# GpSimd waits for the landing of seven gathered blocks one gather later in a graph layer

## Chip, cores and metric

One core of one Trainium2 chip. The metric is the time of one execution on the device, in microseconds (us); less is better. The kernel before took 3305.88 us, the median of 3 runs (3302.12 to 3306.97).

## What is computed

Two layers over 6250 nodes of 256 features (x), in f32. The first, which matters here, is a relational graph layer over 200000 edges, sorted by their end node (dst); each edge has a source node, one of 16 types and a weight:

```python
def _L0_gnn_ref(feat, norm, weight, w_comp, h_bias, loop_weight, src, dst, etypes):
    w_full = jnp.einsum('rb,bdo->rdo', w_comp, weight)
    x_rel = jnp.einsum('nd,rdo->rno', feat, w_full)
    msg = x_rel[etypes, src] * norm
    agg = jax.ops.segment_sum(msg, dst, num_segments=N)
    out = agg + h_bias + feat @ loop_weight
    return jax.nn.relu(out)

    x = x + _L0_gnn_ref(_layernorm(x, axis=-1), edge_weight1, ...)
    x = x + _L0_ffn_ref(_layernorm(x, axis=-1)[None], ...)[0]
```

The second is a mixture of 16 experts of which each node uses 2. The change doesn't touch it.

The end nodes are drawn as 6250 times the square of a uniform number, so low nodes have many more edges than high ones. The host hands the nodes over in reverse order: the kernel meets the sparse end first, and a tile of 256 nodes has few edges at the start of the graph layer and very many at its end.

## The kernel before

The kernel has stages in order: loading and normalising the rows, tables and coefficients of the edges (both before 196 us), the graph layer (`graph_layer`, to about 2699 us), routing, experts, and combining. In the graph layer the edges stand in 1568 blocks of 128. For each block the 128 source rows of 256 f32 (128 KB) are gathered from DRAM (`d.feat`) into a slot of a ring in SBUF, `rows`, of RB = 56 slots. The nodes are in windows of WIN = 16; each pair of a block and a window that it touches is a step, 1960 steps in all, and U = 7 steps are a turn, 280 turns. TW = 16 windows are a tile of 256 nodes.

**GpSimd** issues the gathers (line 1060), one indirect DMA for each block, in sections of GB = 14. Ahead of a section (lines 1043 to 1056) it waits until TensorE has done the turn after which the ring has room for the section (`s_P`, `free[q]`): room means that all blocks more than 42 below the first of the section are used. Then it copies the list of source nodes of the next section (`list_in`, line 1035). Every seven gathers (QB = 7) count their landing on one semaphore, `s_row[at // QB]`, so the ring has eight of them, used in turn; a gather adds 16. Ahead of the first gather of each seven stands `landed` (line 1038), which waits until the seven before have landed, all of them, and then increments `s_paced`. The first 28 gathers are issued in the stage before (line 712), with no such wait, and partly in a run with nothing between them.

**SyncE** waits for the same semaphores in their order, seven blocks after seven, and adds 7 to `s_in` each time (`rows_in`, line 1016).

**VectorE** builds for each turn the matrix S of selected coefficients (line 1147), in four buffers; it waits there for the turn of TensorE that used the buffer last. After the turn that ends a tile it also does the work on the nodes of that tile (`nodes`, lines 1093 to 1117).

**TensorE** goes through the turns. In each it waits for S and for the rows of the turn's blocks (`s_in`), and does 7 products of S with a slot of the ring into PSUM (line 1282; 14 matmul records in the profile). Where a turn is the first of a new tile it does the product of the former tile with the basis weights first (`tile_product`: lines 1211, 1224, 1192, 1232, 1237, 1201). **ScalarE** moves the windows out of PSUM (lines 1340, 1342) and serves the tile products with copies (line 1354).

Of the kernel before, what the change touches and what calls it, by code (L numbers as in the profile page):

```python
# [79 lines left out]
GB = 14  # L80
QB = 7
# [89 lines left out]
def later(i):  # L171

    return not isinstance(i, int) or i > 0
# [784 lines left out]
def graph_layer(nc, d, a, ctl, pairs, room, wend, srcT, dstS, wgtS, coefS, ident, wb, lw, hb, gw, s_w, logit, choice, mean, rstd, idx, rows, s_row):  # L958
# [5 lines left out]
    with ctx:  # L964
# [38 lines left out]
        @blk.sync  # L1003
        def _(e):


            for c in range(HC):
                e.dma_start(wb[:, c, :, :], a["L0_gnn_weight"].rearrange("b (c p) o -> c p b o", p=P)[c, :, :, :]).then_inc(s_w, 16)
            e.dma_start(lw[:, :, :], a["L0_gnn_loop_weight"].rearrange("(c p) o -> p c o", p=P)).then_inc(s_w, 16)
            e.dma_start(hb[:, :], a["L0_gnn_h_bias"].partition_broadcast(P)).then_inc(s_w, 16)  # L1010
            e.dma_start(choice[0][:, :], a["L0_ffn_gate_b"].partition_broadcast(P)).then_inc(s_gb, 16)
            e.dma_start(gw[:, :, :], a["L0_ffn_gate_w"].rearrange("(c p) e -> p c e", p=P)).then_inc(s_w, 16)
            def rows_in(i):
                for q in range(RB // QB):
                    e.wait_ge(s_row[q], 16 * QB * (i + 1))
                    e.sem_inc(s_in, QB)  # L1016
            i0 = 0
            for k, (t, n, i1) in enumerate(CHUNK):
                with e.Fori(i0, i1) as i:
                    rows_in(i)  # L1020
                e.wait_ge(s_S, t + n)
                c = slice(t * U * B, (t + n) * U * B)
                e.dma_start(coefS[:, c], d.coef[:, c]).then_inc(s_late[k], 16)
                i0 = i1
            with e.Fori(i0, NBLK // RB) as i:
                rows_in(i)

        @blk.gpsimd
        def _(e):
            ch = Chain(e, s_pool)  # L1030
            regs = [e.alloc_register(f"room{q}") for q in range(IB)]
            last = NBLK // (IB * GB) - 1

            def list_in(group, q):
                ch.add(e.tensor_copy(idx[:, q * GB:(q + 1) * GB], srcT[:, bass.ds(group * GB, GB)]))

            def landed(i, n):

                e.wait_ge(s_row[n % RB // QB], i * (IB * GB // RB * 16 * QB) + (n // RB + 1) * 16 * QB)
                e.sem_inc(s_paced, 1)  # L1040

            def blocks(i):
                e.load(regs, room[0:1, bass.ds(i * IB, IB)])
                free = [e.snap(r, min_val=1, max_val=TURNS) for r in regs]
                for q in range(0 if later(i) else EG, IB):
                    if later(i) or q >= RB // GB:

                        e.wait_ge(s_P, free[q])
                        e.sem_inc(s_turn, 1)
                    if later(i) or q > EG:  # L1050
                        ch.wait()
                    if q < IB - 1 or not isinstance(i, int) or i < last:
                        list_in(i * IB + q + 1, (q + 1) % IB)
                    else:
                        e.sem_inc(s_turn, 1)
                    for u in range(GB):
                        at = (q * GB + u) % RB
                        if u % QB == 0:
                            landed(i, q * GB + u - QB)
                        e.indirect_dma_start(rows[:, at * H:(at + 1) * H], None, d.feat, bass.IndirectOffsetOnAxis(ap=idx[:, q * GB + u:q * GB + u + 1], axis=0)).then_inc(s_row[at // QB], 16)  # L1060
            e.iota(choice[1][:, :], [[1, X]], base=-X, channel_multiplier=0, allow_small_or_imprecise_dtypes=True).then_inc(s_xno, 1)
            e.iota(node.rearrange("p (m n) -> p m n", m=2), [[1, 2], [2, WIN // 2]], base=0, channel_multiplier=0, allow_small_or_imprecise_dtypes=True).then_inc(s_node, 1)
            blocks(0)
            with e.Fori(1, last) as i:
                ch.base, ch.n = IB * i - EG, 0
                blocks(i)
            ch.base, ch.n = IB * last - EG, 0
            blocks(last)

        @blk.vector  # L1070
# [1003 lines left out]
```

## Time and profile before

| | |
|---|---|
| median of 3 runs | 3305.88 us (3302.12 to 3306.97) |
| the profiled execution, its time | 3305.05 us |
| its span | 3303.3 us |
| mean granted TensorE clock | 0.847 of full speed |
| from the first gather of line 1060 to the start of the last | 197.35 to 2653.84 us |

Engines in the profile: PE is TensorE (PEld its weight loads), DVE is VectorE, ACT is ScalarE, POOL is GpSimd, SP is SyncE; a q behind the name is the engine's queue of instructions. Times are us, or ns where said. A wait is put down to what ended it; "issue" is idle time in which the engine waited for nothing that the profile shows. A gather's own duration on POOL is that of its issuing; its bytes move and land later, and appear as DMA traffic.

### The profile page before, as it was taken

Reading aid. Unit: us, or ns where it says so; the run is one execution under the profiler, and the core shown is the slowest. Engines: PE = TensorE matmul, PEld = TensorE weight load, DVE = VectorE, ACT = ScalarE, POOL = GpSimd, SP = SyncE. Lnnn points to the kernel's source line nnn. Section 1 sums busy time; section 2 is a strip of 40 time slices with the busy share of each in tenths; the row PEclk is TensorE's granted clock in tenths of the full one; section 3 lists DMA queues with packets and bytes.
Section 4 is the critical chain, followed back from the end, with each engine's and each line's share of the span. In section 5 each row is a group of like instructions: output and inputs, shape, how many; then the busy total and the mean of one; then the engine's idle time right before and its main releaser. Section 6 shows DMA issues by size and latency. Waiting matters only on the chain. (4 is left out here: it accounts for less than half of the span.)

```text
span 3303.3 us, 37521 instructions
## 1 busy us (share of the span) xinstructions
PE 2350.0 (71%) x11549; PEld 1960.3 (59%) x11550; DVE 940.6 (28%) x2032; ACT 658.2 (20%) x1539; POOL 1813.9 (55%) x2000
## 2 busy tenths in 40 slices
PE   2489888878778676757756665754744447999987
PEld 1468777666666565545545444543533337999986
DVE  6343232322223212222122121211211235333338
ACT  3232322222112111101110100000100014333336
POOL 0536566565665656666566566665666612555544
PEclk9689999989889888878878777776867779999999
DMA  6243333333333333323333332222322245222236
GB/s 214 85 135 100 104 98 107 95 96 117 96 96 93 113 91 95 96 85 96 104 91 90 89 97 89 86 87 81 92 86 81 83 139 196 70 70 69 69 94 228
DMA packets 146265, 338.61 MB, mean 103 GB/s; under 512 B 36674, under 2 KB 56290, under 8 KB 146051
## 3 DMA queue, kind: packets, MB, share of 16 engines
q0 software_dynamic: 89296, 245.33, 24.9%
q1 hardware_dynamic: 39311, 59.54, 5.2%
q10 hardware_dynamic: 17588, 32.88, 3.0%
q8 instruction: 35, 0.57, 0.1%
q14 instruction: 35, 0.29, 0.0%
HBM read 292.84 MB, written 47.97 MB: 103 GB/s over the span
## 5 line engine op out<-in xcount | busy, mean ns | idle before, releaser
L1060 POOL DMA_INDIRECT rows<-feat,idx x1540 | 1463.0, 950 | 972.6 <-DMA rows<-feat,idx 550.8
L1282 PE MATMUL psW<-rows,S 128*128 x3920 | 1152.4, 463 | 686.2 <-SPq L1016 676.8
L1282 PEld LDWEIGHTS psW<-rows,S 128*128 128x128 f32 x3920 | 919.3, 239 | 915.1 <-issue 729.3
L1147 DVE TENSOR_TENSOR S<-psHere,coefS 128x896 f32<-128x896 f32 x280 | 300.6, 1089 | 1823.6 <-PE psW L1282 1501.0
L1340 ACT COPY z<-psW 128x512 f32<-128x512 f32 x196 | 114.6, 585 | 1827.9 <-PE psW L1282 1294.4
L1237 PE MATMUL psG<-wb,zT 128*128 128x256 f32 (+1 forms) x1600 | 354.0, 379 | 0.5 <-issue 0.5
L1237 PEld LDWEIGHTS psG<-wb,zT 128*128 128x128 f32 (+1 forms) x1600 | 301.0, 188 | 46.6 <-issue 1.2
L1731 PE MATMUL psH<-xT,w1x 128*128 128x128 f32 x1840 | 226.7, 277 | 2.7 <-issue 2.7
L1731 PEld LDWEIGHTS psH<-xT,w1x 128*128 128x128 f32 x1840 | 216.5, 193 | 4.4 <-issue 4.3
L1740 PE MATMUL psO<-w2s,hT 128*128 x912 | 215.7, 379 | 0.0
L1682 POOL DMA_INDIRECT expert_rows<-os,at_rows x114 | 117.3, 1029 | 169.8 <-DVE os L1789 169.8
L1704 ACT ACTIVATE hT<-psH,b1T 128x128 f32<-128x128 f32 x460 | 131.1, 368 | 318.5 <-PE psH L1731 282.2
L1740 PEld LDWEIGHTS psO<-w2s,hT 128*128 128x128 f32 x912 | 164.6, 190 | 17.6
L1678 POOL DMA_INDIRECT xs<-y_rows,at_rows x116 | 115.6, 997 | 100.8 <-POOLq L1410 56.6
L1224 PE MATMUL psZ<-ident,z 128*128 128x128 f32 x784 | 134.3, 325 | 38.4 <-issue 16.6
L1224 PEld LDWEIGHTS psZ<-ident,z 128*128 128x128 f32 x784 | 103.1, 164 | 63.5 <-ACT zT L1354 23.5
L1354 ACT COPY zT<-psZ 128x512 f32<-128x512 f32 x196 | 112.4, 587 | 61.7 <-PE psZ L1224 35.5
L1342 ACT COPY psW<-zero 128x512 f32<-128x512 f32 x196 | 115.6, 590 | 6.2
L1789 DVE TENSOR_TENSOR os<-psO,b_b 128x256 f32<-128x256 f32 x114 | 48.3, 424 | 237.3 <-PE psO L1740 197.8
L1773 DVE COPY w1x<-w1s 128x1024 f32 x116 | 85.4, 736 | 0.0
L1899 PE MATMUL psSum<-g,dg 128*128 128x256 f32 x200 | 55.7, 403 | 16.9 <-DMA g<-expert_rows 16.7
L834 PE MATMUL psC<-wc,hot 128*128 128x64 bf16 x744 | 39.9, 213 | 30.1 <-DVE hot L911 17.0
(284 smaller groups left out, 1463.7 us busy)
## 6 DMA issues: line engine op xcount, KB each, us to landing
rows<-feat,idx POOLq DMA_INDIRECT x1568
g<-expert_rows SPq DMA_DIRECT2D x24, 512.0 KB, 5.7
w1s<-in_L_ffn_w SPq DMA_DIRECT2D x8, 1024.0 KB, 10.0
w2s<-in_L_ffn_w SPq DMA_DIRECT2D x16, 512.0 KB, 9.8
feat<-rows SPq DMA_DIRECT2D x24, 256.0 KB, 3.0
fts<-feat ACTq DMA_DIRECT2D x24, 256.0 KB
h<-in_x ACTq DMA_DIRECT2D x24, 256.0 KB
y_rows<-y ACTq DMA_DIRECT2D x24, 256.0 KB
```

Source lines behind the costliest of these rows:

```text
L1060: e.indirect_dma_start(rows[:, at * H:(at + 1) * H], None, d.feat, bass.IndirectOffsetOnAxis(ap=idx[:, q * GB + u:q * GB + u + 1], axis=0) ...
L1147: e.tensor_tensor(S[h][:, :].rearrange("p (s b n) -> p s b n", s=U, b=B), both[:, h * U:(h + 1) * U, :].unsqueeze(2).to_broadcast([P, U, B ...
L1224: last = e.transpose(to[:, k * P:(k + 1) * P], z[:, w * H + c * P:w * H + (c + 1) * P], ident[:, :])
L1237: last = e.matmul(psG[0:Q, m * H:(m + 1) * H], zT[:, at:at + Q], wb[:, c, b, :], start=False, stop=(c == HC - 1 and b == B - 1))
L1282: last = e.matmul(to[u], S[h][:, u * ZC:(u + 1) * ZC], of[u], start=False, stop=True, skip_group_check=True)
L1340: e.copy(z[:, 2 * k * H:2 * (k + 1) * H], bank).then_inc(s_z, 1)
L1342: e.copy(bank.rearrange("p (w o) -> p w o", w=2), zero[:, :].unsqueeze(1).to_broadcast([P, 2, H])).then_inc(s_clear, 1)
L1678: e.indirect_dma_start(xs[n % XS][:, :], None, d.y, bass.IndirectOffsetOnAxis(ap=at_rows[:, n, 0:1], axis=0)).then_inc(s_in[n % XS], 16)
L1682: e.indirect_dma_start(d.two, bass.IndirectOffsetOnAxis(ap=at_rows[:, n + 4, 1:2], axis=0), os_[n % 2][:, :], None).then_inc(s_out[n % 2], 16)
L1704: last = e.activation(hT[k][:, c * P:(c + 1) * P], psH[k][:, c * P:(c + 1) * P], ACT.Relu, bias=b1T[:, bass.ds(ex * FC + c, 1)])
L1731: last = e.matmul(psH[k][:, f * P:(f + 1) * P], w1x[k][:, c * F + f * P:c * F + (f + 1) * P], xT[k][:, c * P:(c + 1) * P], start=(c == 0), ...
L1740: last = e.matmul(psO[k][:, 0:H], hT[k][:, c * P:(c + 1) * P], w2s[:, bass.ds(ex, 1), c, :].rearrange("p e f -> p (e f)"), start=(c == 0), ...
```

## The change

The landing wait moves from ahead of the first gather of each seven to ahead of the second. It is for the same seven blocks, those before. So when GpSimd waits for them, the first gather of the next seven has been issued; its landing counts on the next semaphore of `s_row`. The first time round, in the section that starts at block 28, the wait is for blocks 21 to 27, as before.

```diff
@@ -1055,8 +1055,8 @@
                         e.sem_inc(s_turn, 1)
                     for u in range(GB):
                         at = (q * GB + u) % RB
-                        if u % QB == 0:
-                            landed(i, q * GB + u - QB)
+                        if u % QB == 1:
+                            landed(i, q * GB + u - 1 - QB)
                         e.indirect_dma_start(rows[:, at * H:(at + 1) * H], None, d.feat, bass.IndirectOffsetOnAxis(ap=idx[:, q * GB + u:q * GB + u + 1], axis=0)).then_inc(s_row[at // QB], 16)
```

## Rows read from the trace of the kernel before

**Rows 1.** The page: span, engines' busy us, and their tenths in 40 slices.

```profile
span 3303.3 us, 37521 instructions
PE 2350.0 (71%) x11549; PEld 1960.3 (59%) x11550; DVE 940.6 (28%) x2032; ACT 658.2 (20%) x1539; POOL 1813.9 (55%) x2000
PE   2489888878778676757756665754744447999987
POOL 0536566565665656666566566665666612555544
PEclk9689999989889888878878777776867779999999
```

**Rows 2.** The page's costliest group: busy, mean ns, idle before, its releaser.

```profile
L1060 POOL DMA_INDIRECT rows<-feat,idx x1540 | 1463.0, 950 | 972.6 <-DMA rows<-feat,idx 550.8
```

**Rows 3.** Waits of all engines: who <- whom: us in total, times, longest.

```profile
PE psW L1282 <- SPq L1016: 676.8, 132, 8.9
POOL rows L1060 <- DMA rows<-feat,idx: 550.8, 219, 5.4
POOL rows L1060 <- issue: 421.8, 1321, 1.2
```

**Rows 4.** Timeline of GpSimd (start, us, what, idle before): first and last gathers.

```profile
197.35 1.00 POOL L1060 DMA_INDIRECT rows<-feat,idx  x1 [0.57 <-issue]
...
2646.35 0.94 POOL L1060 DMA_INDIRECT rows<-feat,idx  x1 [2.55 <-DMA rows<-feat,idx]
...
2653.84 0.95 POOL L1060 DMA_INDIRECT rows<-feat,idx  x1 [0.30 <-issue]
```

**Rows 5.** Timeline of GpSimd, one seven's end and the next one's start.

```profile
1514.39 0.95 POOL L1060 DMA_INDIRECT rows<-feat,idx  x1 [0.30 <-issue]
1515.35 0.20 POOL L1035 COPY idx<-srcT 128x14 int32 x1
1517.92 0.97 POOL L1060 DMA_INDIRECT rows<-feat,idx  x1 [2.37 <-DMA rows<-feat,idx]
```

**Rows 6.** Line 1060 (ns min/median/max, first and last start), and its longest wait.

```profile
L1060 POOL DMA_INDIRECT rows<-feat,idx x1540: 940/946/1438, 197.3 to 2653.8; - x193
...
211.28 0.94 POOL L1060 DMA_INDIRECT rows<-feat,idx  x1 [5.43 <-DMA rows<-feat,idx]
```

**Rows 7.** Stretches: us, busy PE, PEld, DVE, ACT, POOL, then PEclk, DMA share, GB/s.

```profile
1515.90:1516.15 0.25, 0.25 (x3) 0.22 (x2) 0.00 (x0) 0.00 (x0) 0.00 (x0) 1.00 0.60 115
1516.40:1516.65 0.25, 0.25 (x3) 0.22 (x2) 0.00 (x0) 0.00 (x0) 0.00 (x0) 1.00 0.62 246
1516.90:1517.15 0.25, 0.25 (x3) 0.22 (x2) 0.00 (x0) 0.00 (x0) 0.00 (x0) 1.00 0.00 0
147.20:160.95 13.75, 3.30 (x34) 2.31 (x34) 1.70 (x3) 0.37 (x1) 10.40 (x11) 0.50 0.36 105
```

**Rows 8.** Timeline of GpSimd: the first and last of 21 long gaps after a first gather.

```profile
380.56 0.94 POOL L1060 DMA_INDIRECT rows<-feat,idx  x1 [1.23 <-issue]
...
2614.00 0.94 POOL L1060 DMA_INDIRECT rows<-feat,idx  x1 [1.22 <-issue]
```

**Rows 9.** Stretches, columns as above; then line 1282 alone, then line 1060 alone.

```profile
2400.00:2600.00 200.00, 98.87 (x252) 74.60 (x252) 25.95 (x28) 2.35 (x4) 121.24 (x135) 0.70 0.28 83
235.88:555.45 319.57, 281.37 (x1337) 240.04 (x1337) 95.20 (x217) 90.51 (x163) 194.99 (x217) 0.94 0.34 100
...
235.88:555.45 319.57, 141.70 (x616) 121.17 (x616) 0.94 0.34 100
...
235.88:555.45 319.57, 191.92 (x202) 0.94 0.34 100
```

**Rows 10.** Timeline of TensorE: a tile product's start, then the turns behind it.

```profile
288.30 0.63 PE L1211 MATMUL psG<-ident,fts 128*128 128x128 f32 x4 [0.86 <-ACT z L1340]
...
311.02 21.31 PE L1282 MATMUL psW<-rows,S 128*128 x98
```

**Rows 11.** TensorE's largest wait from 235 to 600 us.

```profile
PE psW L1282 <- SPq L1016: 11.9, 3, 5.1
```

## The prediction

> **What bounds the kernel now.** I read the page from its top. The engine shares and the row of 40 slices say that no engine is full over the span: TensorE is busy 71% of it at a granted clock that sags from 0.9 to 0.7, GpSimd 55%, and GpSimd's share stays at 5 to 6 tenths from the third slice to the thirty-second [rows 1]. A busy share that flat, over stages in which TensorE's share falls from 9 to 4 tenths, is that of a pace maker: GpSimd repeats one pattern, and the others follow. I left the chain of work that ended last aside: it reaches back only over the last microseconds. The groups by cost name the pattern: 1540 gathers of line 1060, 1463 us busy and 972.6 us idle before them [rows 2].
>
> The waits split GpSimd's idle time: 550.8 us in 219 waits for the landing of its own gathers, and 421.8 us in 1321 gaps of some 0.3 us between gathers [rows 3]. TensorE's message matmuls (line 1282) waited 676.8 us in 132 waits for SyncE's word of landed rows (line 1016) [rows 3]. Busy and idle together, 1463 + 551 + 422, with some 20 us of index copies, are the whole 2457 us from the first gather to the end of the last, 197.35 to 2654.79 [rows 4]. So GpSimd's stream has no slack: it never stands idle for TensorE, and what is taken out of it comes out of the stage, as long as TensorE can follow.
>
> **One period.** The timeline [rows 5] shows it: a gather takes 0.95 us, the next starts 0.30 us later, so 1.25 us each; after the seventh (start 1514.39) GpSimd stands until the first of the next seven at 1517.92. The 14-wide index copy of every second period (0.20 us) lies inside that wait: it is put down as 2.37 us with a copy [rows 5] and 2.55 us without [rows 4]. The mean wait is 550.8 / 219 = 2.515 us. A quiet period is 6 x 1.25 + 3.5 = 11.0 us; the mean over all, (2646.35 - 197.35) / 219 = 11.18 us [rows 4], has the disturbed ones in it.
>
> **The change, part by part.** It removes nothing and adds no instruction. In each seven the landing wait (wait and the increment that follows it) moves from ahead of gather 1 to ahead of gather 2. Moved past it is one gather with its DMA of 128 rows. The wait on TensorE's turns for room in the ring and the index copy stay ahead of gather 1, so what they protect is unchanged; gather 1 counts on the next semaphore, not on the one waited for. SyncE's order of waits is as before. Queued behind the moved wait on GpSimd are gathers 2 to 7, the next copy and the next turn wait; who waits for those is SyncE's relay and through it TensorE.
>
> *The gain for one period.* The wait ends when the seventh gather of the former seven has landed. Let T be the end of that seventh gather. Before: gather 1 starts at T + 2.5. After: gather 1 starts at T + 0.3 (T + 0.5 with the copy), ends at T + 1.25 (T + 1.45), and gather 2 starts at T + 2.5 in place of T + 2.5 + 1.25. The cover holds: 1.45 is under 2.5, with 1.05 to 1.27 us of waiting left. So a period loses exactly one gather with its gap, 0.95 + 0.30 = 1.25 us, and a quiet one becomes 9.75 us. If a gather grew longer, the left-over wait would cover the first microsecond: the 1540 took 940 to 1438 ns, median 946 [rows 6].
>
> *How often.* 219 waits were paid [rows 3]. In all: 219 x 1.25 = 273.8 us.
>
> *Does the extra gather move the landing?* The trace of before has no eighth gather in flight behind a wait, so this is bounded. The DMA engines' traffic in quarter-microsecond stretches [rows 7] shows for the gather issued at 1514.39 a burst from 1515.9 to 1516.65, 1.5 to 2.25 us after its start, then nothing, and the release at 1517.92: some 1.3 us between the last bytes and GpSimd's next start are receipt and signal. The extra gather, started at T + 0.3 = 1515.65, would have its own burst from 1517.15, after the seventh's bytes. And the stream bears it: within a seven each gather is followed by the next 1.25 us later, and between 147.20 and 160.95 eleven gathers went out with no landing wait among them, 13.75 us, still 1.25 us each, at 105 GB/s [rows 7]. That also excludes that an eighth outstanding gather stalls GpSimd. Best bound: no delay, 0 us. Worst bound: the extra 128 KB go in front of or among the seventh's, one burst, 0.75 us: 219 x 0.75 = 164 us lost again. I take 0, the row that it is nearest to being the run of eleven. The Trainium skill, "DMA: Bandwidth & Descriptors", section "Queues, rings and completion order", says that the semaphore increment of a DMA lands after every earlier write of its DMA engine, across queues; by this only earlier traffic can hold the seventh's landing, never the gather issued behind it, and the sum would stay as it is.
>
> *A second gain.* After the first gather of a seven, 21 times, at every 70th gather from 380.56 to 2614.00, the gap is 1.22 us and not 0.30 [rows 8]. I don't know its cause, but since its period is a multiple of seven it always falls between gathers 1 and 2, just where the wait now goes. There it is covered by the left-over wait of 1.27 us: 21 x 0.92 = 19.3 us. The bounds are 0 (it is added to the wait, or shifts elsewhere) and 19.3; I take 19.3, since its place is counted in gathers and their count is unchanged.
>
> *What is late next: TensorE.* From 1000 us on it has room: busy 99 of 200 us in 2400 to 2600, at a clock of 0.70 [rows 9]; the faster stream asks 13% more. The narrow place is the early stage, where a tile of 256 nodes has few edges and its product is as long as ever: TensorE is busy 281.4 us of the 319.57 from 235.88 to 555.45 [rows 9]. At full clock it needs there: six tile products of 22.7 us (288.30 to 311.02) with 0.86 us ahead of each [rows 10], 141 us, and 616 / 14 = 44 turns [rows 9] of 21.31 / 7 = 3.04 us [rows 10], 134 us; together 275 us. GpSimd issued 202 gathers there [rows 9], 28.9 periods, and would now take 319.6 - 28.9 x 1.25 = 283.5 us. So TensorE follows, by 3%. That VectorE follows too is in the same row: seven turns back to back in 21.31 us with the node work of a tile among them [rows 10]. And GpSimd feels TensorE only through the ring: the section of 14 gathers that starts at block n waits until all blocks below n - 42 are used, so TensorE may fall six periods, 58 us, behind; a tile product and the rows of one turn make it some 23 + 11 = 34. I take 0 us.
>
> *The rest.* After the last gather nothing changes: from its start at 2653.84 [rows 4] the last turns, the last tile, routing, experts and output run as before.
>
> **The sum.** The profiled execution has a span of 3303.3 us and a time of 3305.05 us, 0.8 us under the median of the three runs (3305.88). 3305.05 - 273.8 - 19.3 = 3012.0 us, 8.9% less.
>
> **The rivals.** (1) *TensorE is the bound early.* For it: from 235 to 600 us it waited for landed rows only three times, 11.9 us [rows 11]; its other idle time is its own. If busy time and all other idle time stay (319.6 - 11.9 = 307.7 us against 283.5), it falls 24 us further behind. Against it: the ring has 58 - 34 = 24 us left for just that, and a TensorE that waits less gets more clock. With the ring's reserve already spent it costs all of it: 3012 + 24 = 3036 us. (2) *The landing moves later* by up to the burst of 0.75 us: up to 3012 + 164 = 3176 us. For it: landings do stretch when other transfers run, the first wait of the stage lasted 5.43 us beside the loads of weights [rows 6]. Against it: those transfers were ahead of the gather, this one is behind. (3) *The change does nothing*: the landing is seen only with the traffic of the gather behind it, at T + 1.25 + 2.5. Then wait and gather follow each other as before, 219 x 1.25 us come back, and perhaps the 21 gaps: 3286 to 3305 us, the time of before if the gaps stay. Against it: TensorE is released within the wait of before, with no gather behind, and in the run of eleven no such thing would be seen, so only the order of bursts speaks here. (4) *Slower*: with eight in flight where seven were the rule, a landing comes more than 1.25 us later than now; that is the point from which it decides. Its place is all 219 waits. The only price in the trace is the wait of 5.43 us under heavy traffic, 2.9 us over the mean: (2.9 - 1.25) x 219 = 361 us lost, 3666 us. Against it: the DMA engines are busy a third of the time in this stage [rows 9], not all of it.
>
> **How the numbers follow.** Forecast 3012 us with the 21 gaps hidden or not (3012 to 3031): 0.76. Rival 1, to 3036: 0.09. Rival 2, 3037 to 3176: 0.07. Rival 3: 0.04. Rival 4: 0.04. The range runs from 3003 (the forecast less 0.3%, what executions of one kernel differ by) to 3075: the gaps, rival 1, and of rival 2 the part in which a landing comes up to 0.29 us later (63 / 219). Outside it are the rest of rival 2 and rivals 3 and 4. This kernel's measurement can tell about 0.2% from no change, 6.6 us; the first three cases are faster by more, 0.92; rival 3 is mostly within it, 0.04; rival 4 slower, 0.04.
>
> **What the profile of the changed kernel would show.** The landing waits of line 1060 stay 219 or 220, but sum to about 277 us (1.27 each), not 551. They stand ahead of the second gather of a seven; the first follows the seventh by 0.30 us. A quiet period is 9.75 us. The gathers run from 197 to about 2362 us. No gap of 1.22 us is left. TensorE's wait for line 1016 falls by about 290 us less what its higher clock gives back, and the mean clock rises. The time from the last gather to the end stays 649 us. Rival 1 would show waits of GpSimd for TensorE's turns before 600 us; rival 2 landing waits of over 1.3 us; rival 3 waits of 2.5 us at the new place; rival 4 longer ones. I am wrong if the wait at the new place isn't the old one less 1.25 us, or if TensorE's turns come to hold GpSimd.

## The result: slower by half a per cent, and the rows of after

The changed kernel took 3325.68 us (median of 12 runs, 3295.23 to 3336.5) against 3306.88 us of the kernel before on the same chip (12 runs, 3302.12 to 3312.54): a ratio of 1.0052, 95% interval 1.0035 to 1.0069. It is slower, by half a per cent, where 8.9% less was forecast. The profiled execution took 3326.58 us.

The page of after: span, engines, and tenths in 40 slices, then three of its costliest groups (they answer to [rows 1, 2]).

```profile
span 3324.8 us, 37521 instructions
PE 2383.6 (72%) x11549; PEld 1927.5 (58%) x11550; DVE 941.0 (28%) x2032; ACT 663.1 (20%) x1539; POOL 1814.2 (55%) x2000
PE   2576786678687867687777657675575547999987
POOL 0545445555456566456666664666666612555544
L1060 POOL DMA_INDIRECT rows<-feat,idx x1540 | 1463.0, 950 | 691.5 <-issue 563.6
L1282 PE MATMUL psW<-rows,S 128*128 x3920 | 1105.2, 436 | 399.7 <-issue 302.6
L1035 POOL COPY idx<-srcT 128x14 int32 (+1 forms) x109 | 22.0, 202 | 305.6 <-PE psW L1282 275.3
```

The gathers came close to what was forecast. Their idle time fell from 972.6 us [rows 2] to 691.5, by 281.1 us (forecast: 293.1). But GpSimd's copy of the next list of source nodes, behind the wait for room in the ring, now stands idle for 305.6 us, where it stood idle for 1.2 us before. 305.6 - 281.1 = 24.5 us: the span grew by 21.5. The flat 5 to 6 tenths of GpSimd in [rows 1] have got dents: slices of 4. The mean granted clock of TensorE fell from 0.847 to 0.833, where a rise was forecast.

The waits of after between 197 and 2650 us (who <- whom: us in total, times, longest):

```profile
PE psW L1282 <- issue: 299.0, 277, 6.5
POOL idx L1035 <- PE psW L1282: 275.3, 17, 29.1
...
PE psG L1211 <- issue: 102.4, 13, 21.5
PE psW L1282 <- SPq L1016: 25.7, 6, 6.6
```

The same view of before, with two lines that did not stand in the rows ahead of the prediction:

```profile
PE psW L1282 <- SPq L1016: 668.0, 131, 8.2
...
PE psG L1211 <- issue: 10.0, 10, 1.7
...
PE psW L1282 <- issue: 4.3, 4, 3.5
```

TensorE's wait for landed rows is gone, 668.0 to 25.7 us. In its place stands "issue", 4.3 to 299.0 us at line 1282 and 10.0 to 102.4 at line 1211: TensorE waited for nothing that the profile shows. GpSimd's timeline (start, duration, what, idle before) shows the local pattern as forecast, the pause ahead of the second gather and 9.77 us from one to the next:

```profile
1524.46 0.94 POOL L1060 DMA_INDIRECT rows<-feat,idx  x1 [1.23 <-issue]
...
1534.23 0.94 POOL L1060 DMA_INDIRECT rows<-feat,idx  x1 [1.33 <-issue]
```

TensorE's timeline shows what did not follow. GpSimd stood still from 469.3 to 487.92, its list copy waiting for TensorE, and then gathered again, every 1.25 us:

```profile
484.15 18.29 PE L1282 MATMUL psW<-rows,S 128*128 x84
504.73 1.34 PE L1282 MATMUL psW<-rows,S 128*128 x5 [2.29 <-issue]
...
509.93 0.84 PE L1282 MATMUL psW<-rows,S 128*128 x2 [1.05 <-issue]
511.39 1.01 PE L1282 MATMUL psW<-rows,S 128*128 x2 [0.62 <-issue]
512.82 0.58 PE L1282 MATMUL psW<-rows,S 128*128 x1 [0.42 <-issue]
514.23 0.59 PE L1282 MATMUL psW<-rows,S 128*128 x1 [0.82 <-issue]
```

By these records six turns take 3.05 us each, the pace of [rows 10], 14 us of it beside the new gathers. Then one turn takes from 504.73 to 514.82, 10.1 us, in steps of some 1.4 us, and no matmul of line 1282 follows until the next tile product at 529.22. Rows can't have been missing, since GpSimd had just been stopped by a full ring, and the coefficients S of these seven turns were all built by 494.5.

But the records don't agree with what the other engines did. ScalarE moves windows out of PSUM when the turn that completes them has ended:

```profile
493.41 0.59 ACT L1340 COPY z<-psW 128x512 f32<-128x512 f32 x1 [1.81 <-PE psW L1282]
...
502.83 0.59 ACT L1340 COPY z<-psW 128x512 f32<-128x512 f32 x1 [8.21 <-PE psW L1282]
...
515.70 0.59 ACT L1340 COPY z<-psW 128x512 f32<-128x512 f32 x1 [11.67 <-PE psW L1282]
...
522.71 0.59 ACT L1340 COPY z<-psW 128x512 f32<-128x512 f32 x1 [5.80 <-remote]
...
528.40 0.59 ACT L1340 COPY z<-psW 128x512 f32<-128x512 f32 x1 [4.48 <-remote]
```

"remote" marks an increment of a semaphore beside which the profile has no instruction. VectorE's waits for its four buffers end at the same moments. By the semaphore, the seven turns ended at 487.35, 490.37, 493.39, 502.81, 515.68, 522.69 and 528.38 us: three at the old pace, two of them beside gathers, then four of 9.4, 12.9, 7.0 and 5.7 us. So here the profile puts matmuls up to 20 us ahead of the increment that tells the others of them. Over the whole of after, 181 turns ended a wait of VectorE at line 1147; in 121 of them the increment came over 1.5 us behind the recorded end of the last matmul, 6.5 us in the median and 26 us at most. In the kernel before it was 10 of 158. The two ways of reading agree that TensorE's turns reach the others late. They don't agree on where the time goes, and "issue" on TensorE is to be read with that doubt in all that follows.

### The profile page after: what moved, and what is told of

It reads as the page before. It is cut to its first block and busy times, and to the rows that moved or that the text cites. A ratio compares the mean times of both kernels' runs of the same rounds, so it can differ in the third digit from the quotient of the medians.

```text
span 3324.8 us, 37521 instructions
## 1 busy us (share of the span) xinstructions
PE 2383.6 (72%) x11549; PEld 1927.5 (58%) x11550; DVE 941.0 (28%) x2032; ACT 663.1 (20%) x1539; POOL 1814.2 (55%) x2000
## 5 line engine op out<-in xcount | busy, mean ns | idle before, releaser
L1060 POOL DMA_INDIRECT rows<-feat,idx x1540 | 1463.0, 950 | 691.5 <-issue 563.6
L1282 PE MATMUL psW<-rows,S 128*128 x3920 | 1105.2, 436 | 399.7 <-issue 302.6
L1282 PEld LDWEIGHTS psW<-rows,S 128*128 128x128 f32 x3920 | 841.1, 219 | 658.3 <-issue 469.6
L1237 PE MATMUL psG<-wb,zT 128*128 128x256 f32 (+1 forms) x1600 | 379.4, 393 | 23.4 <-issue 22.8
L1237 PEld LDWEIGHTS psG<-wb,zT 128*128 128x128 f32 (+1 forms) x1600 | 311.9, 196 | 87.0 <-issue 38.1
L1224 PE MATMUL psZ<-ident,z 128*128 128x128 f32 x784 | 169.8, 373 | 86.4 <-issue 56.8
L1224 PEld LDWEIGHTS psZ<-ident,z 128*128 128x128 f32 x784 | 124.8, 191 | 124.8 <-issue 79.9
L1035 POOL COPY idx<-srcT 128x14 int32 (+1 forms) x109 | 22.0, 202 | 305.6 <-PE psW L1282 275.3
L1211 PE MATMUL psG<-ident,fts 128*128 128x128 f32 (+1 forms) x100 | 22.4, 366 | 192.3 <-issue 103.1
L1211 PEld LDWEIGHTS psG<-ident,fts 128*128 128x128 f32 (+1 forms) x100 | 14.9, 187 | 203.9 <-issue 203.9
## 6 DMA issues: line engine op xcount, KB each, us to landing
w1s<-in_L_ffn_w SPq DMA_DIRECT2D x8, 1024.0 KB, 10.1
```

What stands on the lines that cost most here:

```text
L1224: last = e.transpose(to[:, k * P:(k + 1) * P], z[:, w * H + c * P:w * H + (c + 1) * P], ident[:, :])
L1237: last = e.matmul(psG[0:Q, m * H:(m + 1) * H], zT[:, at:at + Q], wb[:, c, b, :], start=False, stop=(c == HC - 1 and b == B - 1))
L1282: last = e.matmul(to[u], S[h][:, u * ZC:(u + 1) * ZC], of[u], start=False, stop=True, skip_group_check=True)
```

## The experiments: what holds TensorE, and on which chip

Theories. **A**: TensorE's work is too much for a period of 9.77 us, on any chip. **C**: the trouble comes from GpSimd running so far ahead of TensorE. **K** (formed after the second batch): under gathers that follow each other with short pauses, TensorE's turns come late though its work is the same, and this belongs to some chips only. The expectations below, which call it a slow supply of instructions, use further letters (B, D, Q, R, W) and explain them on the spot; their theory Q has nothing to do with the chips Q1 and Q2. The runs were made on four chips. On two of them, here **P1 and P2**, the kernel before took 3315 to 3317 and 3314 us; on the other two, **Q1 and Q2**, 3277 and 3280 us. The chip of the result behaves as P (its count of matmuls from 100 to 150 us stands in the section on why the prediction was wrong); whether it is one of the four is not on record. P1 was used twice, with Q1 between, and showed the same kind both times. All ratios are against the kernel before on the same chip.

### A longer pause, no pause, a short lead, less work (P1, kernel before 3316.62 us)

**e1_pad** puts an iota of 1024 words on GpSimd, and a wait for it, ahead of each seven of the changed kernel:

```diff
+if u % QB == 0:
+    e.iota(idle[:, :], [[1, 1024]], ...).then_inc(s_idle, 1)
+    e.wait_ge(s_idle, ...)
+    e.sem_inc(s_idle_ok, 1)
 if u % QB == 1:
     landed(i, q * GB + u - 1 - QB)
```

> The changed kernel, with an iota of 1024 words a partition on GpSimd ahead of the first gather of each seven (a new tile nobody reads), which takes about as long as the change saved, so that a period is again near 11 us, while the eighth gather is still in flight at the landing wait. Theory A (TensorE, once it no longer waits for rows, is held by its own supply of instructions; what matters is that GpSimd's stream is faster): the time is that of before, 3300 to 3330 us, with TensorE's 14 products of a turn again in one run and its issue gaps near the 4 us of before. Theory B (the eighth gather in flight itself slows TensorE's instructions or the landings): the issue gaps of about 300 us on line 1282 stay, and the time is above 3400 us, since the slower stream is added to them.

Measured: 3170.77 us (3166.37 to 3175.73), ratio 0.9566 (0.9549 to 0.9583). More work on the engine that set the pace, and the kernel is 150 us faster than the unpadded one on this chip (c1_after, below). Neither A (3300 us or more) nor B (over 3400) had it. Its GpSimd timeline, then its waits:

```profile
1499.99 1.00 POOL L1062 IOTA idle<- 128x1024 f32 x1
1501.78 0.96 POOL L1067 DMA_INDIRECT rows<-feat,idx  x1 [0.79 <-DMA rows<-feat,idx]
```

```profile
PE psW L1289 <- SPq L1019: 508.0, 104, 7.2
...
PE psW L1289 <- issue: 19.8, 11, 5.9
```

The period is 10.4 us with a pause of 1.8 us. TensorE waits for rows again (508.0 us) and hardly by issue (19.8).

**e2_two** is the kernel before with its wait for the seven before the last, so that the pause disappears:

```diff
 if u % QB == 0:
-    landed(i, q * GB + u - QB)
+    landed(i, q * GB + u - 2 * QB)
```

> The kernel before with its landing wait for the seven blocks before the last seven: up to 14 gathers in flight, nearly nothing to wait for, a period of 8.75 us. Theory A: GpSimd only reaches the wait for TensorE's turns sooner; the time stays within 1% of the changed kernel's 3326 us. Theory B: twice the gathers in flight disturb more than one did, 3400 us or more. Had GpSimd been the only bound, it would be 3305 - 550 = about 2755 us.

Measured: 3680.22 us (3663.44 to 3690.37), ratio 1.1096 (1.1054 to 1.1138), against A's forecast and within B's. The period is 8.75 us wherever GpSimd runs, and it runs far too seldom:

```profile
POOL idx L1035 <- PE psW L1282: 703.1, 28, 34.5
PE psW L1282 <- issue: 576.0, 313, 9.8
```

**e3_lead** lets GpSimd run 14 blocks less ahead (28 in place of 42):

```diff
-e.load(regs, room[0:1, bass.ds(i * IB, IB)])
+e.load(regs, room[0:1, bass.ds(i * IB + 1, IB)])
```

> The changed kernel, in which GpSimd may run at most 28 blocks ahead of TensorE instead of 42 (it waits for the turn that the next section waits for). Theory C (TensorE is slow because GpSimd runs far ahead and stands long in its wait for turns): the issue gaps fall and it is faster than 3326 us. Theory A: gaps as in the changed kernel, 3320 us or more, as GpSimd can store less ahead of a tile product. Theory B: as A.

Measured: 3429.35 us (3410.91 to 3446.38), ratio 1.0335 (1.0284 to 1.0385). Theory C falls: less lead costs 108 us more than the changed kernel on this chip, and TensorE's wait by issue at line 1282 is 384.0 us.

**e4_less_after** is the changed kernel with six of the eight bases left out of the tile product, so its output lacks them:

```diff
-for b in range(B):
+for b in range(B - 2, B):
```

> The changed kernel with 6 of 8 bases left out of each tile product (part of the computation is left out): 24 of each 32 matmuls of line 1237, about 10.6 us of TensorE a tile, 265 us in all if TensorE is the bound. Theory A: TensorE is the bound and its instructions are fewer, so the time falls by 200 us or more, towards the 3012 us of GpSimd's own pace. Theory B: the slow issue stays, the time falls by less than 100 us. Its partner, the kernel before with the same left out, is to come: there GpSimd is the bound and it should stay near 3300 us.

Measured: 3161.7 us (3151.8 to 3196.56), ratio 0.9524 (0.9498 to 0.955). TensorE is what GpSimd waits for, so less work on it helps, 160 us against the changed kernel on this chip (c1_after, below). But its wait by issue is not less:

```profile
PE psW L1282 <- issue: 391.1, 324, 6.5
```

The gain is less than A's 200 us and more than B's 100. An engine with too much work should have no idle time of 391 us at its matmuls. That speaks against A, as far as the records can be trusted.

### The other kind of chip (Q1, kernel before 3277.11 us)

**e5_less_before** leaves the same six bases out of the kernel before.

> The kernel before with 6 of 8 bases left out of each tile product (the same part of the computation is left out as in e4). GpSimd's stream of gathers is the bound there, so all theories expect it within 1% of the kernel before less what follows the last gather, some 3290 to 3305 us. Should it fall by 100 us or more, TensorE was the bound of the kernel before too, and the first reading of its profile was wrong.

Measured: 3264.61 us (3264.11 to 3265.85), ratio 0.9959 (0.9943 to 0.9975). As forecast by every theory, TensorE's work is covered in the kernel before: 12 us.

**e6_half** gathers 512 bytes a row in the changed kernel; half of the features are left out, and the ring is zeroed once ahead of it all:

```diff
-e.indirect_dma_start(rows[:, at * H:(at + 1) * H], None, d.feat, ...)
+e.indirect_dma_start(rows[:, at * H:at * H + H // 2], None, d.feat.rearrange("n (a f) -> (n a) f", a=2), ...)
```

> The changed kernel with gathers of half rows: as many descriptors and as many gathers, 512 bytes each in place of 1024, so half the traffic (half of each row's features is left out of the messages). Theory D (bytes on the DMA engines or in the memory hold up the other engines' instructions): the issue gaps of line 1282 fall from 300 to under 150 us and the time to 3200 us or less. Theory Q (it is the issuing of gathers one after the other, with short pauses, whatever they move): the time stays at 3300 to 3340 us.

Measured: 2963.79 us (2962.13 to 2965.44), ratio 0.904 (0.9022 to 0.9058). The pause falls to 1.01 us, the period to 9.49. TensorE waits 482.2 us for rows.

**e7_pad512** is e1_pad with 512 words in place of 1024.

> The changed kernel with an iota of 512 words ahead of each seven, half that of e1: the period should be some 9.9 us, the pause between the last gather of a seven and the next gather some 1.2 us and the second pause, at the landing wait, shorter than the 1.3 us of the changed kernel. Theory Q says that one long pause is needed: with e1's 1.8 us it was enough, so here the time lies between 3171 and 3326 us, or above. Theory R (only the rate of the stream counts, and the slow state begins where TensorE stops waiting for rows): 3100 to 3150 us if that point isn't reached at 9.9 us, about 3300 us if it is.

Measured: 3042.63 us (3038.2 to 3045.7), ratio 0.9283 (0.9268 to 0.9299). The timeline gives a period of 9.86 us with one pause of 0.57 + 0.79 = 1.36 us; the landing wait ahead of the second gather costs nothing any more. Theories Q and R, which had 3171 us or more and 3100 us or more, both missed. TensorE waits for rows, and by issue only 4.0 us, in two waits, at line 1289:

```profile
1508.74 0.57 POOL L1062 IOTA idle<- 128x512 f32 x1
1510.09 0.95 POOL L1067 DMA_INDIRECT rows<-feat,idx  x1 [0.79 <-POOL idle L1062]
```

```profile
PE psW L1289 <- SPq L1019: 529.1, 120, 8.4
```

**e8_even** tries to spread the pause: the landing wait two sevens back, and an iota of 64 words with its wait ahead of every gather.

> The landing wait for the seven before the last, so that nothing waits there, and a short iota with its wait ahead of every gather: gathers evenly spaced at about 1.5 us, a period near 10.4 us as in e1, but without a long pause. Theory R: as e1, 3150 to 3200 us. Theory Q: the other engines never get a long pause, TensorE's issue gaps are at least those of the changed kernel, and the time is 3330 us or more.

Measured: 3936.77 us (3934.45 to 3936.96), ratio 1.2005 (1.1985 to 1.2025). It was mis-sized: the wait of GpSimd for its own iota costs more than the iota.

```profile
1500.38 0.20 POOL L1061 IOTA idle<- 128x64 f32 x1
1501.36 0.96 POOL L1066 DMA_INDIRECT rows<-feat,idx  x1 [0.79 <-POOL idle L1061]
```

Each gather takes some 1.96 us, a seven 13.7 us, and the kernel is bound by rows. It tells nothing of the theories.

That this chip showed hardly an issue wait under a period of 9.49 us was not foreseen, and gave theory K. Three further batches test it.

### The changed kernel again, and the pause in steps (P1, kernel before 3314.78 us)

> The changed kernel itself, beside the kernels that follow, since the comparison of e1 to e4 and that of e5 to e8 had different times of the kernel before (3317 and 3277 us). Theory K (the slow supply of instructions belongs to some chips, not to the kernel alone): where the kernel before is near 3277 us, this one is near 3030 us with no issue gaps on line 1282; where it is 3305 to 3317 us, it is near 3326 us with gaps of 300 us. Theory W (a landing wait with a gather in flight disturbs, an iota doesn't): near 3326 us, or at least 150 us above c3, on any chip.

> The kernel of e2 again (wait for the seven before the last). Theory K: where the kernel before is near 3277 us, GpSimd's pace of 8.75 us a period or TensorE's own work bounds it, 2750 to 2900 us; on the other kind of chip 3600 us or more as in e2. Theory W: it doesn't wait for landings at all, so it should have been fast in e2 too, and W is already in trouble there; 3680 us again on any chip.

> The kernel of e7 again (iota of 512 words ahead of each seven, period 9.86 us, no real landing wait left). Theory K: 3043 us where the kernel before is near 3277 us; where it is 3305 to 3317 us, issue gaps come and the time is between 3171 (e1, 10.35 us) and 3326 us. Theory W: near 3043 to 3080 us on any chip.

> The kernel of e1 again (period 10.35 us). Theory K: where the kernel before is near 3277 us about 3130 us (3277 less 219 times 0.67 us), with no issue gaps; else 3171 us again. Theory W: 3130 to 3171 us on any chip.

Measured: **c1_after**, the changed kernel, 3321.45 us (3289.94 to 3350.01), ratio 0.9995 (0.9965 to 1.0026). **c2_two** (as e2_two) 3668.68 us, 1.107 (1.1047 to 1.1093). **c3_pad512** (as e7_pad512) 3230.4 us (3211.82 to 3265.57), 0.9729 (0.9697 to 0.9761), 188 us more than on Q1; its TensorE waits 208.2 us by issue and 188.7 us for rows. **c4_pad1024** (as e1_pad) 3158.09 us, 0.9529 (0.951 to 0.9549). Theory W, which had the 512-word version at 3043 to 3080 us on any chip, falls.

### The same kernels on two more chips (P2, kernel before 3314.03 us; Q2, 3279.56 us)

> The changed kernel once more. Theory K (the slow supply of instructions to TensorE belongs to some chips): on a chip where the kernel before takes about 3277 us, the changed kernel takes some 3030 us (the 512-word version took 3042.6 there, with a period of 9.86 us against 9.77 us), TensorE waits for VectorE's S by issue under 20 us in sum and GpSimd's idx waits for TensorE under 50 us. On a chip where the kernel before takes about 3310 us: 3320 us again. Theory A (TensorE's work alone is too much for a period of 9.77 us, on any chip): 3250 to 3330 us on either chip.

> The changed kernel with gathers of 512 bytes a row in place of 1024 (half of the features are left out). Where the kernel before takes about 3310 us: if it is the bytes of the gathers that slow the supply of instructions to TensorE, the time is about 2965 us as it was on the other chip (2963.8 us), with hardly a wait by issue; if it is the issuing itself, whatever its bytes, the period of 9.5 us brings at least what the 9.86 us period brought there (3230 us) or more, and TensorE's waits by issue are over 100 us. Where the kernel before takes about 3277 us: 2964 us again.

> The kernel before with its wait two gathers later (period 8.75 us while GpSimd stands for nothing else). Theory K: on a chip where the kernel before takes about 3277 us there are hardly any waits by issue, TensorE's own work (turns of 3.04 us) bounds, and the time is 2950 to 3080 us. Where the kernel before takes about 3310 us: 3670 us again. Theory A: over 3500 us on either.

> The changed kernel with an iota of 1024 words and its wait ahead of the first gather of each seven (period about 10.4 us). Where the kernel before takes about 3277 us: period 10.4 against 11.0, 219 periods, so some 130 us less: about 3145 us, slower than the 512-word version's 3042.6 there. Where the kernel before takes about 3310 us: 3160 us again.

Measured on P2: **d1_after** 3402.16 us (3380.96 to 3414.16), ratio 1.0243 (1.0205 to 1.0281). **d2_half** 3524.93 us (3482.33 to 3540.88), 1.0651 (1.0612 to 1.069). **d3_two** 3672.65 us, 1.1088 (1.1062 to 1.1113). **d4_pad1024** 3168.39 us, 0.9559 (0.9541 to 0.9577). The surprise is d2_half: the kernel that took 2963.79 us on Q1 takes 3524.93 here, and more than the changed kernel itself with twice its bytes. The waits of d2_half:

```profile
POOL idx L1035 <- PE psW L1282: 448.3, 27, 34.6
PE psW L1282 <- issue: 365.7, 296, 6.6
```

So it isn't the bytes of the gathers. With half of them the landing comes sooner and the pause gets shorter (1.05 us), and the kernel is slower. Of the two cases expected for such a chip it is that of the issuing itself.

> The changed kernel once more. If the slow supply of instructions belongs to the chip (theory K): on a chip where the kernel before takes about 3277 us some 3030 us, with TensorE's waits by issue under 20 us; where the kernel before takes about 3310 us, 3320 to 3400 us again. If the changed kernel is slow by itself (theory A): over 3250 us on both.

> The changed kernel with gathers of 512 bytes a row (half of the features are left out), which took 2963.8 us on the one chip and 3524.9 us on the other. Theory K: one of these two times again, by the chip: 2964 us where the kernel before takes about 3277 us, 3525 us where it takes about 3310 us. If the two differed by something other than the chip, the time lies elsewhere or on the other side.

Measured on Q2: **f1_after** 3022.61 us (3017.2 to 3024.11), ratio 0.9216 (0.9201 to 0.9231). **f2_half** 2954.32 us (2953.75 to 2956.83), 0.9008 (0.8993 to 0.9024). Theory K stands, as far as it says that the slow turns belong to some chips, and A falls: the changed kernel, unchanged to the letter, is 7.8% faster on this chip and no faster on P. Its page (span, group of line 1060), its waits between 160 and 2364 us, and line 1060 alone (ns min/median/max, first and last start):

```profile
span 3015.4 us, 37521 instructions
...
L1060 POOL DMA_INDIRECT rows<-feat,idx x1540 | 1463.4, 950 | 721.6 <-issue 451.1
```

```profile
PE psW L1282 <- SPq L1016: 514.1, 114, 8.2
...
PE psW L1282 <- issue: 1.9, 5, 0.8
POOL rows L1060 <- PE psW L1282: 0.6, 2, 0.3
```

```profile
L1060 POOL DMA_INDIRECT rows<-feat,idx x1540: 940/946/1543, 157.9 to 2363.9; - x193
```

GpSimd waits for TensorE 0.6 us in all, and TensorE waits 514.1 us for rows and 1.9 by issue.

The whole, by the longest pause of a seven:

| pause, period of a seven | kernel | P1, P2 (before 3314 to 3317) | Q1, Q2 (before 3277, 3280) |
|---|---|---|---|
| 2.5 of 11.0 us | before | 3315 | 3278 |
| 1.8 of 10.4 | 1024 words | 3171, 3158; 3168 | |
| 1.36 of 9.86 | 512 words | 3230 | 3043 |
| 1.3 of 9.77 | the change | 3321; 3402 | 3023 |
| 1.0 of 9.5 | the change, half the bytes | 3525 | 2964; 2954 |
| 0.3 of 8.75 | two sevens back | 3680, 3669; 3673 | |

On Q a shorter period is a shorter time, in the four rows that were run there. On P the time has its least, of the pauses tried, at 1.8 us. The executions of one kernel scatter too: the changed kernel by 1.8% on P1 (3290 to 3350 us) and by 0.2% on Q2.

### What the traces of the two kinds hold

The traces settle more than the times. Ahead of the first gathers the kinds are alike: from 60 to 80 us TensorE is busy 15.38 us on the chip of the result and 15.39 on Q2, with 323 and 325 GB/s moved. The first indirect gather, of line 723, starts at 84.53 us in before and at 85.41 in f1_after; some 10 us behind it they part. Behind the last gather they are alike again: 649.5 us to the end in before, 651.5 in f1_after. So these chips aren't slower in general.

The profile itself is disturbed in the same place. The increments of semaphores that the packed traces hold are 1035, 1024 and 1024 before 84 us, in before, after and f1_after. From 200 us to 60 us behind the last gather, where the three kernels make nearly the same ones, they are 15660, 9005 and 28971 (e2_two, with no pause, has 6927). Of the 280 ends of a turn the trace of before holds 228, that of after 253, that of f1_after all, each within 0.01 us of its last matmul where VectorE waited for it. And in the waits of the two kinds (before, after between 197 and 2650 us; f1_after has no such line):

```profile
ACT z L1340 <- remote: 126.4, 21, 18.6
```

```profile
ACT z L1340 <- remote: 797.3, 75, 52.4
```

On P much of the record is lost beside gathers, and the more so the shorter their pauses. That leaves a rival that no run tests: every time on record stands beside a span and a clock that were recorded with it, so the writing of the record may itself be what holds the engines on P. Whether the kinds differ in an execution that isn't recorded is not shown.

## Why the prediction was wrong, step by step

**The gain for one period** held. Period 9.77 us, pause 1.23 to 1.33 where 1.27 was left over, no landing later. In f1_after the second gather starts 2.57 and 2.59 us behind the end of the seventh, where the first did 2.58 and 2.55 us behind it before. Rivals 2, 3 and 4 did not occur, on either kind of chip.

**A second gain** was wrong. The 21 gaps at every 70th gather are not covered by the wait but added to it. From f1_after's GpSimd timeline, the two ordinary pauses around one of them:

```profile
1506.57 0.94 POOL L1060 DMA_INDIRECT rows<-feat,idx  x1 [1.23 <-DMA rows<-feat,idx]
...
1516.36 0.94 POOL L1060 DMA_INDIRECT rows<-feat,idx  x1 [1.34 <-DMA rows<-feat,idx]
...
1527.83 0.94 POOL L1060 DMA_INDIRECT rows<-feat,idx  x1 [2.93 <-issue]
```

2.93 us at 1527.83, and about that at 21 places 70 gathers apart. It is 1.60 us over an ordinary pause of 1.33, where before the gap was 0.92 us over an ordinary one. So where 19.3 us were to be won, (1.60 - 0.92) x 21 = 14 us were lost, outside the prediction's bounds of 0 and 19.3. With this the forecast for Q is nearly whole: the idle time of line 1060 goes from 972.6 us in before to 721.6, 251.0 less; 273.8 - 14 = 260 were to be had, and the 9 us that remain are 0.04 us a period (9.79 us, not 9.75). The kernel's own gain there is 3279.56 - 3022.61 = 257.0 us. Of 293.1 forecast, 257 came.

**What is late next: TensorE** is the step that failed, and the whole of the wrong sign comes from it. It took TensorE's need as 44 turns of 3.04 us and six products, 275 us in a stretch for which GpSimd would take 283.5, and gave 0 us. The work was sized right: Q2 does it. What was wrong is that a turn of 3.04 us, read from a trace in which GpSimd paused 2.5 us in every 11, was taken as a property of TensorE alone. On P the turns take longer as those pauses shrink, four of seven 5.7 to 12.9 us in the stretch shown above, and GpSimd stood 305.6 us for them where the prediction had 0. Stretches of 200 us (busy and count of PE, PEld, DVE, ACT, POOL, then clock, DMA share, GB/s), from the kernels before, after, e2_two and f1_after in this order:

```profile
600.00:800.00 200.00, 160.76 (x710) 134.24 (x710) 51.38 (x112) 46.99 (x83) 121.16 (x134) 0.89 0.34 103
```

```profile
600.00:800.00 200.00, 150.49 (x696) 125.14 (x695) 50.74 (x111) 45.20 (x81) 104.24 (x116) 0.90 0.29 87
```

```profile
600.00:800.00 200.00, 133.08 (x587) 110.02 (x585) 48.13 (x108) 43.23 (x76) 101.66 (x114) 0.80 0.28 83
```

```profile
600.00:800.00 200.00, 168.04 (x796) 141.84 (x795) 52.72 (x114) 46.93 (x86) 133.69 (x149) 0.95 0.37 113
```

GpSimd has 149 instructions through on Q2 where it has 116 on the chip of the result, fewer than the 134 of before, and TensorE 796 matmuls against 696. (At 600 us Q2 is further on in the work, so the counts are a measure of pace, not of the same turns.) The clock, 0.90 against 0.95, is too small a difference for it, and the DMA engines are less busy, 0.29 against 0.37.

**Rival 1** had the right mechanism, GpSimd held by TensorE's turns before 600 us, and the sentence "I am wrong if TensorE's turns come to hold GpSimd" came true. Its price was the mis-sized term: 24 us, since it let TensorE's own idle time stay as it was; what was measured is 305.6 us of GpSimd's idle at line 1035. The ring's reserve of 58 us doesn't help against a rate; it is spent once.

**The row that was missed** stands in the trace of before. The prediction looked at a run of gathers with no landing wait among them to see whether the gathers keep their pace. It did not ask whether the others keep theirs. From 84 us on the stage of lines 712 and 723 sends such gathers. Stretches of 50 us, columns as above, of before, of e5_less_before (which has the same code up to there, on Q1) and of f1_after (Q2):

```profile
100.00:150.00 50.00, 30.45 (x444) 26.32 (x444) 23.77 (x58) 19.50 (x58) 21.92 (x24) 0.74 0.25 72
```

```profile
100.00:150.00 50.00, 40.52 (x842) 33.84 (x839) 41.35 (x84) 31.92 (x104) 32.22 (x34) 1.00 0.61 170
```

```profile
100.00:150.00 50.00, 41.04 (x831) 34.71 (x827) 40.69 (x83) 31.55 (x101) 31.68 (x34) 0.97 0.60 171
```

It is the same program, at the same place in it at 84 us, and yet 444 matmuls against 842 (after has 449, so its chip is of the kind P). Before's trace alone would not have given the 842, but it did show GpSimd standing for TensorE there, the pattern that the change then spread over the graph layer:

```profile
POOL edge L723 <- PE psT L808: 22.9, 6, 4.4
```

It also accounts for why the kernel before is faster on Q: in e5_less_before the gathers of line 1060 start at 157.8 us, not at 197.35 [rows 4], 39.5 us earlier. Their stream, paced by pauses, is 9 us longer there (157.8 to 2623.1, 2465.3 us, against 2456.5). The difference, 31 us, is nearly the 30 us that part the chip of the result from Q1 (3306.88 and 3277.11). P1 and P2 are 7 to 10 us slower still, and no trace of before is kept from them.

**The 0.92 for faster** came from cases that all took place on one assumed chip. A case "TensorE's turns come later when the gathers come closer" was not among the rivals. Slower was rival 4 alone, at 0.04 and by another mechanism.

**What stays open.** Why the turns come late, and even whether the matmuls start late, end late, or only their increments do. The expectations call it a slow supply of instructions; no run shows that. The Trainium skill, "Runtime: NRT & Kernel Launch", section "Instruction fetch mechanics", says that each engine refills its store of instructions by DMA, and that this is mostly hidden. The traces agree as far as they go: the instruction queues carry 35 packets each in before, after and f1_after, and those of queue 8 take 1.10, 1.07 and 1.05 us in the mean, so neither more reloads nor longer ones are seen where it is slow. The writing of the record, named above, is the rival that nothing here tests, and no run shows what differs between the chips. VectorE is touched too: its waits by issue at line 1139 grew from 37.5 to 60.0 us. It is also open why the change and the 512-word version, alike in pause and period within 0.1 us, are 91 us apart on P1 (3321 and 3230 us), and whether a pause between 1.36 and 1.8 us would be still better there. That the changed kernel is faster on P with an iota of 1024 words and its wait put in is shown three times (e1_pad, c4_pad1024, d4_pad1024); that the length of the pause alone does it is not, since those 91 us lie between two kernels of nearly one pause.

## What to carry to other kernels

An engine's pace read from a trace holds for the company it had in that trace: before a stream that runs beside it is made denser, look for a stretch in which it is already dense, and count what the other engines get done there. Where the gain of a denser stream comes back as idle time of the others, a wait put back into the stream can be worth more than it costs: with a pause of 1.8 us a seven, the kernel was 4.3 to 4.7% faster on both chips P. Run a change on more than one chip before a verdict: this one is worth 0.9216 on one and 1.0243 on another. And where a program on one core shows waits ended by "remote", compare the records of an engine with what the engines behind it did: its own timeline may be 20 us off.

## What the hardware did that was not expected

- Chips of one type differ by more than the change: the kernel with 512-byte gathers took 2954 and 2964 us on two chips and 3525 us on a third, while the kernel before differs by 27 to 40 us between the kinds.
- Under gathers with pauses of 1.3 us a seven, turns of TensorE that take 3.05 us reached the other engines after 5.7 to 12.9 us on the chip of the result. Its matmul records run ahead of that by 6.5 us in the median and 26 us at most; on Q2 they agree within 0.01 us.
- Of the increments of semaphores in the graph layer, the traces hold 9005 of the changed kernel there and 28971 on Q2.
- GpSimd's wait for its own iota costs 0.79 us beyond the iota, whether of 64 words (0.20 us) or of 512 (0.57 us); an iota of 1024 words takes 1.00 us.
- A gap of 1.22 us at every 70th gather of line 1060 isn't covered by a landing wait at the same place but lengthens it, from 1.33 to some 2.93 to 3.0 us. Its cause is not known.
